# Layer-norm output h handled one chunk later, GpSimd's copy held until the sixth split, narrow matmul operands 258 wide

## What is computed

```
h = max(layernorm(x), 0)
x = x + relu(A_norm @ (A2 @ h @ W.T))      # A2 = adj + I, A_norm = A2 scaled by its diagonal
h = max(layernorm(x), 0)
x = x + softmax(cos(h@Wg, h@Wg) + log(adj + 1e-8)) @ (h @ Wg) + bias
h = max(layernorm(x), 0)
x = x + relu(normalised adj @ h @ W2 + b2) # normalised by the row sums of adj
h = max(layernorm(x), 0)
h = relu(concat(h, adj @ h) @ W1); h = relu(concat(h, adj @ h) @ W2); x = x + h
```

## Time and profile before

| | us |
|---|---|
| median of 3 runs | 2486.02 |
| lowest and highest | 2483.68, 2486.75 |
| span of the profiled execution | 2484.0 |
| TensorE busy | 2434.0 (98%) |
| VectorE busy | 1462.1 (59%) |
| ScalarE busy | 1145.1 (46%) |
| GpSimd busy | 143.5 (6%) |

### The profile page before, as it was taken

The page is one execution under the profiler, slowest core; times in us unless marked ns, Lnnn a source line. Parts: engine busy times, 40 slices in busy tenths (PEclk is TensorE's granted clock), DMA queues, the critical chain, the costliest instruction groups (busy, mean ns, idle before and its releaser), DMA issues.

```text
span 2484.0 us, 43195 instructions
## 1 busy us (share of the span) xinstructions
PE 2434.0 (98%) x17096; PEld 1640.3 (66%) x17096; DVE 1462.1 (59%) x1899; ACT 1145.1 (46%) x1435; POOL 143.5 (6%) x114
## 2 busy tenths in 40 slices
PE   7999999999999999999999999999999999999999
PEld 6888887656666767777888666666544444555555
DVE  7655555666666566666777665566544444455555
ACT  6544443555555544444444444444434334343433
POOL 2300000111110000000000010001000000000000
PEclk9999999999999999999999999999999999999999
DMA  5455555545454766676676544444455455456564
GB/s 204 154 202 188 201 195 194 187 169 178 176 178 158 205 181 201 213 244 206 217 241 231 187 170 169 169 171 167 169 180 186 175 179 184 177 198 219 209 218 170
DMA packets 113727, 473.23 MB, mean 191 GB/s; under 512 B 14432, under 2 KB 47456, under 8 KB 72672
## 3 DMA queue, kind: packets, MB, share of 16 engines
q1 hardware_dynamic: 113344, 471.13, 55.5%
q10 hardware_dynamic: 288, 0.79, 0.1%
HBM read 438.32 MB, written 33.55 MB: 190 GB/s over the span
## 4 chain that ended last, share of the span: by engine, by line
issue 66%; PE 26%; POOL 5%; DMA 1%; DVE 1%; ACT 1%; POOLq 0%; SPq 0%; ACTq 0%; DVEq 0%
PE acc L472 8%; PE acc L483 4%; PE acc L485 4%; PE acc L484 4%; PE acc L473 4%; POOL rstd L417 3%; POOL own L431 1%; DMA adj<-in_adj_t 1%; DVE alo L1036 1%; ACT ahi L789 1%; PE psS L594 0%; PE psS L592 0%; PE psS L593 0%; POOL d L450 0%; PE psW L592 0%
## 5 line engine op out<-in xcount | busy, mean ns | idle before, releaser
L1036 DVE SCALAR_TENSOR_TENSOR alo<-adj,ahi 128x2048 f16<-128x2048 f32 x320 | 743.5, 2323 | 683.0 <-ACT ahi L789 683.0
L472 PE MATMUL acc<-mov,ahi 128*128 128x512 f16 x3072 | 1002.4, 379 | 26.4 <-DVE alo L1036 26.4
L789 ACT ACTIVATE ahi<-adj 128x2048 f16<-128x2048 f32 x320 | 610.9, 1909 | 716.9 <-PE acc L473 337.5
L473 PE MATMUL acc<-mov,alo 128*128 128x256 f16 x3072 | 837.3, 273 | 0.0
L475 PE MATMUL acc<-mov,ahi 128*128 128x257 f16 x2048 | 558.1, 273 | 4.3 <-DVE alo L1036 2.4
L476 PE MATMUL acc<-mov,ahi 128*128 128x256 f16 x2048 | 560.9, 274 | 0.0
L477 PE MATMUL acc<-mov,alo 128*128 128x257 f16 x2048 | 556.2, 272 | 0.0
L472 PEld LDWEIGHTS acc<-mov,ahi 128*128 128x128 f16 x3072 | 300.5, 98 | 386.6 <-DVE alo L1036 32.0
L473 PEld LDWEIGHTS acc<-mov,alo 128*128 128x128 f16 x3072 | 300.6, 98 | 34.5
L475 PEld LDWEIGHTS acc<-mov,ahi 128*128 128x128 f16 x2048 | 196.8, 96 | 46.2 <-DVE alo L1036 4.4
L476 PEld LDWEIGHTS acc<-mov,ahi 128*128 128x128 f16 x2048 | 197.9, 97 | 39.4
(11 more groups left out here) (109 smaller groups left out, 1965.3 us busy)
## 6 DMA issues: line engine op xcount, KB each, us to landing
adj<-in_adj_t SPq DMA_DIRECT2D x320, 1024.0 KB, 4.8
adj<-in_adj_t SPq DMA_DIRECT2D x128, 512.0 KB, 4.8
sent<-expo SPq DMA_DIRECT2D x112, 256.0 KB, 2.8
expo<-sent SPq DMA_DIRECT2D x56, 512.0 KB, 5.1
xres<-in_x SPq DMA_DIRECT2D x7, 512.0 KB, 9.9
out<-xres SPq DMA_DIRECT2D x7, 512.0 KB, 6.5
xres<-in_x ACTq DMA_DIRECT2D x1, 512.0 KB, 3.3
shared<-in_w3a SPq DMA_DIRECT2D x1, 512.0 KB, 6.5
```

The costliest lines, as they stand in the source:

```text
L472: nc.tensor.matmul(acc[:, b, :].rearrange("p (s n) -> p s n", s=2), hi, both, start=first, stop=False)
L473: return nc.tensor.matmul(acc[:, b, 0:F], lo, m[:, jb, 0:F], start=False, stop=last)
L789: nc.scalar.activation(ahi[:, c % 2, :, :], adj[:, c % 2, :, :], ACT.Copy, scale=ADJ_SCALE)\
L1036: nc.vector.scalar_tensor_tensor(alo[:, c % 2, :, :].rearrange("p b n -> p (b n)"), adj[:, c % 2, :, :].rearrange("p b n -> p (b n)"), ADJ ...
```

## The change

**Tables.** `h` goes from chunk 3 to chunk 4 on ACT and DVE; on DVE `norm` stays in chunk 3. On ACT, T0 goes from chunk 4 to 5. On PE, T0 goes from behind the last block row of chunk 3 to behind the first of chunk 4, W0 and T1 from (4, 0) to (4, 2), W1 from (5, 0) to (5, 1), G0 from (6, 0) to (6, 1) and G1 from (6, 2) to (6, 3), the end of chunk 6. **GpSimd.** `own` of a group waits for that group's split 5. **Width.** The 257-column matmuls of passes 0 and 2 become 258 wide; the new column is the second column of ones, and nothing reads its result.

```diff
+OWN = 5
...
                     if not (isinstance(g, int) and p == 0):
                         pool.wait_ge(sum_ready, at(SELF, p, g, 1, 0))
+
+                    pool.wait_ge(split_ready, chunk_no(p, g, OWN) + 1)
                     rows = mov[p % 2][:, bass.ds(g * GB, GB), :]
...
-                n = F + 1
+                n = LO
...
-            PLACES = {(3, 3): "T0", (4, 0): "W0T1", (5, 0): "W1", (6, 0): "G0", (6, 2): "G1"}
+            PLACES = {(4, 0): "T0", (4, 2): "W0T1", (5, 1): "W1", (6, 1): "G0", (6, 3): "G1"}
...
-            PLACES = {0: ["ev"], 3: ["h"], 4: ["T0"], 5: ["W0", "T1", "n0"], 6: ["W1", "n1"], 7: ["g0", "g1"]}
+            PLACES = {0: ["ev"], 4: ["h"], 5: ["T0", "W0", "T1", "n0"], 6: ["W1", "n1"], 7: ["g0", "g1"]}
...
-            PLACES = {0: ["ev"], 1: ["epi"], 2: ["x", "stats"], 3: ["norm", "h"], 5: ["W0", "n0"], 6: ["W1", "n1"]}
+            PLACES = {0: ["ev"], 1: ["epi"], 2: ["x", "stats"], 3: ["norm"], 4: ["h"], 5: ["W0", "n0"], 6: ["W1", "n1"]}
```

## The result

The changed kernel takes 2456.45 us (median of 4 runs, 2455.99 to 2459.20), the kernel before 2485.28 (4 runs, one more than when the prediction was made). The ratio is 0.9886, with a 95% interval of 0.9872 to 0.9900: 28.8 us less, where 32.7 were forecast. The profiled execution's span is 2455.0 us, 29.0 under the one of before.

The account below looks back on a forecast made before the run. TensorE, busy 98% of the span, was taken as the bound. 28.0 + 4.2 - 3.9 + 4.4 = 32.7 us off the 2484.0 span gives 2451.3; runs' median lies 2.0 above: 2453.3 us, range 2448 to 2461.

Parts of the forecast that it names:

- The stands behind T0: TensorE idle at chunk 4's start in groups whose tail has a layer norm; claimed removed, 28.0 us together.
- The slacks: Pass 1's time to spare in the new order: 0.7 us at lo(4), 0.9 at T0, 1.2 at W0, none at W1.
- The group spacings: Distance between successive groups after the change: 46.7 us in pass 1, 47.75 in pass 3.
- rival 5: Stands move elsewhere, as lo(4) waits for norm and norm for rstd: +6 us, 2459; chance 0.12 shared with another rival.
- part 2: GpSimd's own put behind split 5, so lo(2) is no longer slowed in pass 0; 4.2 us gained.
- The new stand at the start of pass 1's groups: G1's later copy delays hi(0), so TensorE waits for ev's first addition: 0.64 us in 6 groups, 3.9 given back.
- I take the second: Passes 0 and 2: chose odd width as the excess's cause, so 258 columns cost 329.2 ns a block, -2.1 ns.
- The term of -4.4 us: Gain from 258 columns in passes 0 and 2, 1024 blocks each, TensorE the bound in both.
- the 3.0 ns: Pass 0's time per block that is not columns: 331.3 ns against 327.5 plus 0.8; blamed on odd width.
- Rival 1: Passes 0 and 2: width brings nothing or costs its column; 2457.7 us, up to 2459.4; chance 0.25.
- the sum: Whole kernel: all gains less what is given back, 32.7 us off the span, for a time of 2453.3 us.

## Why the prediction was right, and where it was not

**The stands behind T0.** Right in place, number and size: 16, 28.0 us, all gone. The slacks held; at the thinnest, W1, TensorE lost 0.02 us a group, in seven groups (its input was forecast to be there 0.03 us before it). The group spacings came as forecast, 46.68 against 46.7 and 47.74 against 47.75. In rival 5 one sum is off: with norm 0.12 us ahead and a slack of 0.7, an rstd 1 us later overdraws it by 0.2 and not 0.4, 3 us and not 6. It moves neither the range nor the time forecast.

What the prediction took as given is how long rstd takes. In the earlier trace rows it starts 0.17 us behind lo(3) and runs 2.99 us; so it does, at 2.98 or 2.99, ahead of all 16 stands. With no split beside it the same operation takes 1.01, as at the start of the program before the change:

```profile
33.80 1.01 POOL L417 TENSOR_TENSOR rstd<-vare,neghalf 128x4 f32<-128x4 f32 x1 [6.31 <-DVE vare L1126]
```

The 1.97 us more are what own lost, too, when it began 0.18 us behind a split. So by the traces a good part of the late h was the same exclusion as part 2's, with GpSimd as the one that waits. An estimate from the earlier trace rows: had rstd ended 1.97 us earlier and all behind it followed, TensorE would have gone on at 604.36, ahead of the 604.52 at which T0 is through, and there would have been no stand. No run here moved rstd, so this is not shown; the change leaves rstd at 2.99 and takes it off the path.

**The new stand at the start of pass 1's groups.** Forecast 0.64 us, 6 times, by VectorE's first addition of `ev`; measured 0.63, 6 times, by that line. Moving G0 and G1 one block row forward took 3.8 us off and the six stands with it. That shows that the cause is what follows G0 and G1 in ScalarE's queue ahead of hi(0); that it is g1's is read from the timeline.

**own.** Forecast 4.2; the trace has 4.2, the runs of the part alone 3.6 (interval 1.7 to 6.2).

**The width.** This step failed, "I take the second, since the even widths (256, 512) all fit one line and the odd one alone is off it". The term of -4.4 us was 0. The two points that made the line have multiples of 256 columns, and the one that was off it differed from them in two things, in being odd and in being over 256. The odd column costs its pair's other half, 0.83 ns a block for two matmuls, and 258 pays that in full; the rest of the 3.0 ns is not oddness. Rival 1 is what happened, at its lower price: 2457.7 forecast, 2456.45 measured. The prediction named nothing against it and still gave it half the chance of its own value. The Trainium skill's gap of columns over 2.4 GHz plus about 2.5 ns would have made the part +1.7 us ("TensorE: Matmul & The Clock Gate", "Back-to-back issue gap"). It is nearer than my value, and near from 258 to 260 and on to 264, but it has no pairs: from 257 to 258 it says 0.42 ns a matmul, 0.83 a block, and the blocks say 0. The same section calls this the gap of a single matmul by itself and gives about 131 ns for 512 columns in a stream with weight loads; the stream of pass 1 has 216 ns, so for that width it is the formula that holds here.

**The remainder.** With the width at 0 the sum gives 2457.7, and 1.25 us below that were measured. Of these 0.75 are in the spans (28.3 forecast, 29.05 found): the start's clock, 1.7 us less in the profiled execution after, against pass 5's transfers, 0.8 more. The other 0.5 are the medians, which lie 2.0 us above the span before and 1.5 after. None of this was in the prediction, and none belongs to the change. That the forecast missed by 3.2 us and not by the 4.4 of the failed term is luck.

## What to carry to other kernels

Where a stage waits for a far engine, put it in the queue behind the work that the bottleneck needs next, and move every engine's share of the stage with it: with TensorE's places left as they were two thirds of the gain was lost. Then look at the far end of the stage, since a shift by one block there can put a copy ahead of the next group's first split. Where two elementwise operations exclude one another as the split does with own and rstd, start the long-awaited one first, or move the other into a gap. What that gains is the stand that the overlap caused, 0.57 us here, and not the whole 1.38 by which the split was longer. Last, a price for a width that no row has is a guess, even if two points lie on a line.

## What the runs showed of the hardware

- Moving columns (fp16) are paid in pairs: 331.36 and 331.36 ns a block at 257 and 258 columns, 333.13 and 333.13 at 259 and 260.
- VectorE's fp32 split and GpSimd's addition exclude one another, and which of them pays is decided by 0.2 to 0.4 us of head start (3.67 us for a split of 2.29, or 3.87 for an addition of 1.90). The loser waits 0.14 us less than the other one's remaining time, both ways.
- GpSimd's rstd of 128 x 4 takes 2.98 us when it starts 0.17 us behind a split, and 1.01 alone. In the attention of the kernel before it took 1.38 to 1.42 behind VectorE's product of adj and `expo`, both in SBUF, and 1.01 behind that of adj and `psS`, which is in PSUM, four times each. A split of the attention (L1255) that began 0.42 us into such an rstd still took its usual 0.68.
- At the same place of the program, behind the same pause of some 2 us, TensorE fell to 1.2 GHz for part of a stretch in some executions (granted 0.52 to 0.71 in 31.0 to 34.2 us in seven of the twelve traces) and stayed at 2.4 GHz in the other five (granted 1.00). Between the traces before and after this is 1.7 us.
